# Two heads per step in the narrow query tiles of a causal pooled attention

## What is computed

```python
k_sem2, k_geo2, v2 = (pool(k_sem), pool(k_geo), pool(v))      # 48 pooled + 1024 keys
scores = q_sem @ k_sem2 / sqrt(32) + q_geo @ k_geo2 / sqrt(32)  # times exp(logit_scale)
scores = jnp.where(mask, scores, NEG_INF)
probs = jax.nn.softmax(scores, axis=-1)
x = x + (probs @ v2) @ Wo
# then, with xn = layernorm(x):
y = square(relu(xn @ up_w)) @ down_w + (xn @ expert_weight) * (sum of the top 2 of xn @ gate_w)
x = x + layernorm(y)
```

## Time and profile before

| what | us |
|---|---|
| median of the 2 runs shown | 2548.39 |
| their lowest and highest | 2512.27, 2584.51 |
| the profiled execution's own time | 2502.36 |
| its span, slowest of the cores (2489.0 to 2500.8) | 2500.8 |

### The profile page before, as it was taken

The page is one execution under the profiler, slowest core; times in us unless marked ns, Lnnn a source line. Parts: engine busy times, 40 slices in busy tenths (PEclk is TensorE's granted clock), DMA queues, the critical chain, the costliest instruction groups (busy, mean ns, idle before and its releaser), DMA issues.

```text
span 2500.8 us, 32154 instructions; the slowest of 8 cores (2489.0 to 2500.8 us)
## 1 busy us (share of the span) xinstructions
PE 1756.3 (70%) x8936; PEld 889.1 (36%) x8936; DVE 612.4 (24%) x1264; ACT 562.9 (23%) x1289; POOL 162.1 (6%) x290
## 2 busy tenths in 40 slices
PE   0566666655555566554649989999997999999800
PEld 0444444322232233222523434444443444444400
DVE  4332332132345655353020000000000000000065
ACT  1222223423446655212431111111110000000200
POOL 0111111000000000000000000000000000000023
PEclk9756556767655555676759999999998999999855
DMA  9532320310400000231005654444444454454123
GB/s 225 105 92 68 100 70 2 101 34 1 77 1 3 16 1 1 85 118 68 1 8 113 141 92 77 76 76 76 76 76 76 101 110 85 85 108 103 76 101 134
DMA packets 46786, 185.08 MB, mean 74 GB/s; under 512 B 6560, under 2 KB 10912, under 8 KB 37152
## 3 DMA queue, kind: packets, MB, share of 16 engines
q0 software_dynamic: 27744, 86.02, 20.5%
q1 hardware_dynamic: 18880, 97.00, 12.1%
HBM read 243.86 MB, written 25.17 MB: 108 GB/s over the span
## 4 chain that ended last, share of the span: by engine, by line
PE 61%; issue 11%; DVE 10%; ACT 8%; DMA 6%; POOL 1%; another core or an unknown queue 1%; DVEq 1%; ACTq 0%; SPq 0%; POOLq 0%
PE PSA L1043 18%; PE PSA L1009 18%; ACT arena L456 4%; PE PSA L985 4%; PE PSA L540 3%; PE PSA L449 3%; PE PSA L695 3%; PE PSA L567 3%; PE PSA L823 2%; PE PSA L858 2%; DVE arena L776 2%; DMA arena<-xq 2%; PE PSA L802 2%; PE PSA L907 2%; DMA arena<-we 1%
## 5 line engine op out<-in xcount | busy, mean ns | idle before, releaser
L1043 PE MATMUL PSA<-arena 128*128 128x512 bf16 x2048 | 443.5, 380 | 17.7 <-DMA arena<-wd 17.7
L1009 PE MATMUL PSA<-arena 128*128 128x512 bf16 x2048 | 444.7, 380 | 8.5 <-DMA arena<-wu 8.5
L1043 PEld LDWEIGHTS PSA<-arena 128*128 128x128 bf16 x2048 | 200.7, 98 | 260.6 <-issue 19.9
L1009 PEld LDWEIGHTS PSA<-arena 128*128 128x128 bf16 x2048 | 200.8, 98 | 252.4 <-issue 12.5
L449 PE MATMUL PSA<-identb,arena 128*128 128x128 bf16 x960 | 119.4, 277 | 172.8 <-DVE arena L679 56.0
L456 ACT CAST arena<-PSA 128x512 bf16<-128x512 f32 x256 | 149.8, 585 | 191.6 <-PE PSA L449 177.4
L1018 DVE TENSOR_TENSOR arena<-arena 128x1024 bf16<-128x1024 bf16 x64 | 44.3, 692 | 568.3 <-ACT arena L1014 568.3
L802 PE MATMUL PSA<-arena 128*128 128x128 bf16 (+1 forms) x448 | 84.4, 299 | 131.5 <-DVE stat L793 32.2
L1014 ACT ACTIVATE arena<-PSA 128x1024 bf16<-128x1024 f32 x64 | 65.5, 1023 | 387.7 <-PE PSA L1009 387.7
L449 PEld LDWEIGHTS PSA<-identb,arena 128*128 128x128 bf16 x960 | 76.4, 118 | 211.7 <-issue 206.1
L540 PE MATMUL PSA<-arena 128*128 128x256 bf16 x512 | 108.9, 402 | 40.6 <-DMA arena<-wk 23.7
(11 more groups left out here) (113 smaller groups left out, 1419.9 us busy)
## 6 DMA issues: line engine op xcount, KB each, us to landing
arena<-xb SPq DMA_DIRECT2D x16, 2048.0 KB, 10.2
arena<-wu POOLq DMA_DIRECT2D x64, 512.0 KB, 5.1
arena<-wd POOLq DMA_DIRECT2D x32, 1024.0 KB, 13.7
arena<-xq SPq DMA_DIRECT2D x4, 2048.0 KB, 10.2
arena<-xq SPq DMA_DIRECT2D x8, 1024.0 KB, 8.4
x1sp<-arena SPq DMA_DIRECT2D x8, 1024.0 KB, 5.8
arena<-we POOLq DMA_DIRECT2D x16, 512.0 KB, 6.3
moesp<-arena SPq DMA_DIRECT2D x16, 512.0 KB, 6.9
```

Of the source, the lines that this page charges most:

```text
L1009: items = [(lambda e, k=k, seg=seg, sl=sl, pb=pb: e.matmul(pv(512 * pb, 512), wub[sl].rearrange("p (k c) -> p k c", k=KD)[:, k, :], xn2Tv[ ...
L1043: items.append(lambda e, kp=kp, wsl=wsl, seg=seg, pb=pb: e.matmul(pv(512 * pb, 512), wdb[wsl].rearrange("p (k c) -> p k c", k=32)[:, kp % ...
```

## The change

Tiles with at most 512 key columns are worked two heads at a time. Tasks become triples (tile, first head, number of heads): 8 tasks for each of tiles 1 to 5 and 16 for each of the others, 88 in all. For a pair:

- st1 puts the two heads' scores into two PSUM banks;
- st2 takes the minimum with the mask for both in one instruction over a 128x2x64 view, with the mask repeated by a zero stride, then one negate and accumulate for both, so that the pair has one common row maximum; one exponential for both, without accumulation; and a new reduce_sum on VectorE, which sums each head's 64 exponentials;
- st3a takes both reciprocals in one instruction, makes two diags, two transposes into one bank and one copy of 256 columns;
- st3b does two value products side by side in bank 7 and two output copies.

The number of diag buffers goes from two to four. Tiles 0, 6 and 7 are worked as before. Apart from this, the first load back from `moesp` waits for the last two stores besides its own.

```diff
-        diagb = [av(32 * K + i * 512, 128, BF16) for i in range(2)]
+        diagb = [av(32 * K + i * 512, 128, BF16) for i in range(4)]
...
+            tasks = []
+            for j in range(NQT):
+                if WJ[j] <= 512:
+                    for t in range(8):
+                        tasks.append((j, 2 * t, 2))
+                else:
+                    for h in range(H):
+                        tasks.append((j, h, 1))
...
+                    E('vector', lambda e, sview=sview, bview=bview, nview=nview: e.tensor_tensor(
+                        out=nview, in0=sview, in1=bview, op=ALU.min),
+                      reads=sbanks + [f'bmv{bs}'], writes=[f'negS{hp}'])
...
+                E('vector', lambda e, hp=hp, wt=wt: e.tensor_scalar(
+                    out=negS[hp][:, 0:wt], in0=negS[hp][:, 0:wt], scalar1=-1.0, scalar2=3e38,
                     op0=ALU.mult, op1=ALU.min, accum_out=stat[:, 2 + hp:3 + hp]),
                   reads=[f'negS{hp}'], writes=[f'negS{hp}', f'st_negmax{hp}'])
...
+                if nh == 2:
+                    E('scalar', lambda e, hp=hp, wt=wt: e.activation(
+                        out=Pb[hp][:, 0:wt], in_=negS[hp][:, 0:wt], func=AF.Exp,
+                        bias=stat[:, 2 + hp:3 + hp], scale=-1.0),
+                      reads=[f'negS{hp}', f'st_negmax{hp}'], writes=[f'Pb{hp}'])
+                    E('vector', lambda e, hp=hp, w=w: e.reduce_sum(
+                        stat[:, 90 + 2 * hp:92 + 2 * hp],
+                        Pb[hp][:, 0:2 * w].rearrange("p (h k) -> p h k", h=2),
+                        axis=mybir.AxisListType.X),
+                      reads=[f'Pb{hp}'], writes=[f'st_rowsum{hp}'])
...
+                    E('vector', lambda e, hp=hp: e.reciprocal(stat[:, 35 + 2 * hp:37 + 2 * hp],
+                                                              stat[:, 90 + 2 * hp:92 + 2 * hp]),
+                      reads=[f'st_rowsum{hp}'], writes=[f'st_recip{hp}'])
+                    for hh in range(2):
+                        E('vector', lambda e, hp=hp, hh=hh: e.tensor_scalar(
+                            out=diagb[2 * hp + hh], in0=identb[:],
+                            scalar1=stat[:, 35 + 2 * hp + hh:36 + 2 * hp + hh], scalar2=None,
+                            op0=ALU.mult),
+                          reads=['identb', f'st_recip{hp}'], writes=[f'diag{2 * hp + hh}'])
+                    items = [(lambda e, hh=hh, hp=hp, w=w: e.matmul(
+                        pv(6 * 512 + 128 * hh, 128, 0, w),
+                        Pb[hp][:, hh * w:hh * w + w], diagb[2 * hp + hh],
+                        start=True, stop=True)) for hh in range(2)]
+                    MMG(items, [f'Pb{hp}', f'diag{2 * hp}', f'diag{2 * hp + 1}'], ['bank6'])
+                    E('scalar', lambda e, pq=pq: e.copy(
+                        out=PTs[pq][:, 0:256], in_=pv(6 * 512, 256)),
...
+                    E('scalar', lambda e, m=m, j=j: e.copy(
+                        out=OTv[0:64, m, 128 * j:128 * (j + 1)], in_=pv(7 * 512, 128, 0, 64)),
+                      reads=['bank7'], writes=['OT'])
+                    E('scalar', lambda e, m=m, j=j: e.copy(
+                        out=OTv[64:128, m, 128 * j:128 * (j + 1)],
+                        in_=pv(7 * 512 + 128, 128, 0, 64)),
+                      reads=['bank7'], writes=['OT'])
...
                 E('sync', lambda e, dm=dm: e.dma_start(out=moer[0], in_=moesp[dm]),
-                  extra=[ms_evs[dm]], dma=True, slot='mr0', writes=['moer0'])
+                  extra=[ms_evs[dm]] + (ms_evs[-2:] if dm == 0 else []),
+                  dma=True, slot='mr0', writes=['moer0'])
```

More of the change, by code:

```diff
@@ L774, in st2 @@
                 bs = j % 2
[L775 to L780, removed]
+                sbanks = [f'bank{b}' for b in range(sA * 3, sA * 3 + max(1, (wt + 511) // 512))]
@@ L787, in st3a @@
             def st3a(i):
-                j, h = flat[i]
+                j, h0, nh = tasks[i]
                 w = WJ[j]
@@ L792, in st3a @@
                 kts = kt_list(w)
[L793 to L808, removed]
-                      reads=['bank6'], writes=[f'PTs{pq}'])
@@ L810, in st3a @@
-                if dbg and j == 0 and h == 0:
+                if nh == 2:
+                    E('vector', lambda e, hp=hp: e.reciprocal(stat[:, 35 + 2 * hp:37 + 2 * hp],
[14 more added lines that the diff above has]
+                        out=PTs[pq][:, 0:256], in_=pv(6 * 512, 256)),
+                      reads=['bank6'], writes=[f'PTs{pq}'])
+                else:
+                    E('vector', lambda e, hp=hp: e.reciprocal(stat[:, 6 + hp:7 + hp],
+                                                              stat[:, 4 + hp:5 + hp]),
+                      reads=[f'st_rowsum{hp}'], writes=[f'st_recip{hp}'])
+                    E('vector', lambda e, hp=hp: e.tensor_scalar(
+                        out=diagb[2 * hp], in0=identb[:], scalar1=stat[:, 6 + hp:7 + hp],
+                        scalar2=None, op0=ALU.mult),
+                      reads=['identb', f'st_recip{hp}'], writes=[f'diag{2 * hp}'])
+                    for k0 in range(0, len(kts), 4):
+                        kn = min(4, len(kts) - k0)
+                        items = [(lambda e, kt=k0 + ii, ii=ii, hp=hp, kts=kts: e.matmul(
+                            pv(6 * 512 + 128 * ii, 128, 0, kts[kt]),
+                            Pb[hp][:, 128 * kt:128 * kt + kts[kt]], diagb[2 * hp],
+                            start=True, stop=True)) for ii in range(kn)]
+                        MMG(items, [f'Pb{hp}', f'diag{2 * hp}'], ['bank6'])
+                        E('scalar', lambda e, k0=k0, kn=kn, pq=pq: e.copy(
+                            out=PTs[pq][:, 128 * k0:128 * (k0 + kn)], in_=pv(6 * 512, 128 * kn)),
+                          reads=['bank6'], writes=[f'PTs{pq}'])
@@ L811, in st3a @@
+                if dbg and j == 0 and h0 == 0:
                     E('gpsimd', lambda e, hp=hp: e.dma_start(out=DBG['d_p'][:, 0:WJ[0]],
@@ L815, in st3b @@
             def st3b(i):
-                j, h = flat[i]
+                j, h0, nh = tasks[i]
                 w = WJ[j]
-                kv = h // 4
-                m = h // 2
-                half = h % 2
                 pq = i % 3
                 kts = kt_list(w)
[L823 to L827, removed]
@@ L836, in build_program @@
+            for step in range(NTASK + 3):
+                if step < NTASK:
                     st1(step)
-                if 0 <= step - 1 < NH:
+                if 0 <= step - 1 < NTASK:
                     st2(step - 1)
-                if 0 <= step - 2 < NH:
+                if 0 <= step - 2 < NTASK:
                     st3a(step - 2)
-                if 0 <= step - 3 < NH:
+                if 0 <= step - 3 < NTASK:
                     st3b(step - 3)
```

88 lines of the change are left out of this document (62 added, 26 removed).

## The result

| | before | after |
|---|---|---|
| median of all runs, us | 2508.67 (10 runs, the two shown earlier among them) | 2532.37 (11 runs) |
| profiled execution, us | 2502.36 | 2532.41 |
| span, slowest core | 2500.8 | 2530.9 |

The ratio of the runs is 1.0104, 95% interval 1.0093 to 1.0115: slower beyond doubt, and within 2%. Some runs of a program on all eight cores are disturbed and some per cent longer; they are left out of the ratio, and one such run had lifted the median of the two runs shown earlier from about 2508 to 2548.

A forecast was written before the change was run, and what follows sets the result against it. Bound by the order of waits, no engine full. Nine loop terms sum to 3.53 us per narrow pair against 2.70; 40 pairs give +33: 2535.6 on the profiled execution, 2545 on the lower run. Predicted 2540, range 2508 to 2600.

The forecast's parts named there:

- The sum: Narrow pair steps: loop terms add to 3.53 us per pair against 2.70, over 40 pairs +33 us.
- How the numbers follow: Closing part, whole run: +33 gives 2535.6 on the profiled execution, 2545 on the lower run; predicted 2540, range 2508 to 2600.
- The baseline: Narrow heads before the change: 78 steps in 105.34 us, so 1.35 us per head and 2.70 per pair.
- the two loops of the kernel before: Single narrow heads: VectorE's start-to-start chain 1.43 us; a loop over two steps 2.55, or 1.28 per step.
- The loop: Pair step: reduce_sum waits for its own task's exponential, so the two-step loop closes within one step, 3.53 us per pair.
- this alternative: Reduce on VectorE at two columns per cycle: the sum would be shorter by an estimated 0.06 us per pair.
- What was at nothing: Second score matmul, diag buffers, one-head tasks in tiles 6 and 7 (at most 2 us), moer load's wait: all left out.
- Grouping pays: Rival, VectorE's queue in the pair step: VectorE's own order sets 1.98 us per pair, -29 us, 2473; chance 0.07.
- The pairs don't pipeline: Rival, pair step: a second matmul costs 0.34 like a lone one, 4.01 us per pair, +52 us, 2555; chance 0.16.
- its two terms: Pair step, transposes to value products and value products to first output copy: each grows by 0.24 us in that rival.
- Only exponential and reduce in the loop: Rival, pair step: ScalarE's older copies clear in time, 2.80 us per pair, +4 us, 2506, no difference; chance 0.12.

The follow-up runs named there:

- the kernel with one head per step: Kernel before, but in tiles 1 to 5 a VectorE reduce_sum behind the negation replaces the exponential's accumulated row sum; ratio 1.0392, stage 305.4 us.
- the load's wait: Kernel before with only the other edit: the first load back from moesp also waits for the last two stores; ratio 1.0004, stage 207.7 us.
- the late reduce: Changed kernel with only the reduce_sum moved to st3a, just ahead of the reciprocal, one step after its exponential; ratio 0.9868, stage 175.9 us.
- values-first kernel: Changed kernel with value products and output copies emitted ahead of transposes and their copy in pair steps; ratio 0.9986, stage 207.6 us.
- interleaved kernel: Kernel with the reduce one step late, its VectorE order in pair steps alternating instructions of two successive tasks; ratio 0.9853, stage 175.3 us.

## Why the prediction failed, and where it held

**The number went the wrong way.** The sum said +33 us, the text said slower but within 2%, and the kernel became 26 us slower, within 2%; 2532 also lies in the range. But the single time I gave, 2540, lies below the median shown, 2548.4, so as a forecast of the median it says faster, which is the opposite of my own sum. The step that failed is in "How the numbers follow": I added the shift to the profiled execution (2502.4) and to the lower of two runs, chose a time between the two results, and used the shown median only for the high end of the range. A shift has to be carried on the number that it is a shift of, or the text has to say that this number is itself expected to move. Two runs 72 us apart could not carry a forecast of 33; ten put the median at 2508.7, and 2508.7 + 33 would have been 2542 against 2532.4 measured: 9 us too high, of which the baseline and the loop's terms below make some 6 (40 x 0.07 and 40 x 0.09).

**The baseline was miscounted.** Between 758.99 and 864.33 there are 76 steps, not 78: the minimum at 758.99 is the fourth narrow one, not the second. These stand ahead of it in the kernel before:

```profile
745.97 0.23 DVE L776 TENSOR_TENSOR arena<-PSA,arena 128x64 f32<-128x64 f32 x1 [1.80 <-ACT arena L829]
...
751.71 0.23 DVE L776 TENSOR_TENSOR arena<-PSA,arena 128x64 f32<-128x64 f32 x1 [3.45 <-ACT arena L829]
...
757.06 0.23 DVE L776 TENSOR_TENSOR arena<-PSA,arena 128x64 f32<-128x64 f32 x1 [4.13 <-PE PSA L802]
```

From the fourth of 80 to the last it is 76 steps, which makes 1.39 us per head and 2.77 per pair, not 2.70. With it the same sum gives 40 x (3.53 - 2.77) = +30. It also loosens the trust in such sums: the two loops of the kernel before, 1.43 and 1.28, lie 0.04 above and 0.11 below the 1.39 measured.

**The loop was right, two terms too long.** In the prediction's order, forecast and measured in the turn shown above (the second diag starts at 801.97, inside the merged row of L835):

| term | forecast | measured |
|---|---|---|
| second diag to transposes | 0.51 | 0.50 |
| transposes to value products | 0.45 | 0.34 |
| value products to first output copy | 0.54 | 0.55 |
| first to second output copy | 0.34 | 0.35 |
| second output copy to exponential | 0.28 | 0.28 |
| exponential to reduce | 0.60 | 0.57 |
| reduce to reciprocal | 0.26 | 0.20 |
| reciprocal to first diag | 0.33 | 0.33 |
| first to second diag | 0.22 | 0.25 |
| sum | 3.53 | 3.37 |

The second transpose does not push the value products back: they start 0.34 behind the first transpose, as behind a lone one. That the second transpose fits into a distance that is there anyway is a reading; no run separates it. From reduce to reciprocal the prediction took 0.29 less an overlap that it read from the pair L779 and L793; that pair shows none (0.24 apart, L779 takes 0.22), and the diag of the earlier trace rows does (0.17 apart, 0.25 long), which would have given 0.21. The mean spacing is 3.44, not 3.37, since some steps are longer (last section). 40 x (3.44 - 2.77) = +27, measured +25.6; the difference is that the first three pairs and the last don't run at this spacing. The reduce took 0.286, forecast 0.29. Against the 0.220 for half the columns, in the kernel with one head per step, 64 more columns cost 0.066, 1.03 ns each, as they do for L776. That is the one-per-cycle mode of the Trainium skill ("VectorE: DVE Perf Modes", perf-mode tier table); at half of that the reduce would have taken 0.23, so this alternative is excluded.

**What was at nothing was nothing:** the load's wait (its own experiment) and tiles 6 and 7 (137.7 us from the first 576-column minimum to the last minimum in both). The diag buffers and the second score matmul have no run of their own; the loop as measured leaves no time for them.

**The rivals.** Grouping pays: not as the change was made, but the mechanism is real, the late reduce gives -32 us in the stage where the rival's working said -29, with the same 1.98 per pair, to which its terms add up by luck (reduce to reciprocal 0.39, not 0.26; negation to reduce 0.21, not 0.28). It lay as close as one line's place in the source. "The pairs don't pipeline" is refuted: its two terms would have been 0.69 and 0.78, and they are 0.34 and 0.55. "Only exponential and reduce in the loop" did not occur. The values-first kernel comes near that case: there the transposes and their copy bring the exponential 1.31 us behind the second diag, and minimum and negation would bring it after 1.29 (0.31 + 0.48, and the 0.50 from negation to exponential of the interleaved kernel). It came out at no difference, stage 0.0, where the rival's working said +4. The rule quoted from the Trainium skill ("Perfetto Trace Analysis", Optimizing Scalar/DVE Operations), that grouping pays where an engine is saturated, points the right way for the change as it was made. But measured against the same kernel before, with its VectorE 62% busy, the same grouping paid 31.7 us in the same stage once the reduce was emitted a step later. The order of the queues decided, not saturation.

## What to carry to other kernels

In a software pipeline on in-order engines, look not at what an added instruction costs but at what it waits for and what is queued behind it: an instruction that reads another engine's result of the same step, placed ahead of older work, turns a loop over two steps into one over one step. Emit the consumer one step late, beside the other work of that age. Before giving a time, carry the shift onto the very number that it is compared with, and count the steps in a stretch from the list of their starts.

## What the hardware showed that I had not expected

- VectorE makes a gap of about 0.35 us at regular places of its queue, whatever stands there. Two of them, in the changed kernel and in the kernel before:

```profile
798.59 0.26 DVE L835 TENSOR_SCALAR arena<-identb,stat 128x128 bf16<-128x128 bf16 x1 [0.34 <-DVE arena L835]
```

```profile
799.96 0.16 DVE L793 RECIPROCAL stat<-stat 128x1 f32<-128x1 f32 x1 [0.33 <-issue]
```

  In time they lie some 19 us apart in the changed kernel, 15 with the values first, and 11 with the late reduce and in the kernel before. In work it is always the same: eight single heads or between five and six pairs, which is 125 to 131 of VectorE's records in the trace, counting also those that the views leave out. So they go by the number of instructions, not by time. With the late reduce each gap lengthens a step, from 1.98 to 2.33 at the most. In the changed kernel only three of six do (at 798.59, 818.54 and 856.56); the others fall where VectorE has time to spare. The rest of the 0.07 by which its mean spacing lies above a regular step is in steps longer by 0.14 to 0.2 us, with gaps on TensorE and ScalarE, and in the first two. What causes the gaps is open; no run tried it.
- Two value products written to different partitions of PSUM start together (both at 801.81), while side by side in the same partitions they started 0.09 apart; the copy behind them came 0.08 earlier.
